# A two-layer decoder on one core: its first stages reordered, gate products turned round, out_proj and the next norm in one stage

## The reference

```python
x = x + mamba_int8(ln(x))       # in_proj, conv of 4 taps, x_proj, dt, scan over 512 tokens, out_proj; all weights and
                                # activations rounded to int8 steps: qa(x, s) = clip(round(x / s), -128, 127)
x = x + cross_attention(ln(x), ctx)   # 16 heads of 128, rms-normed q and k; softmax; out
x = x + sparse_experts(ln(x))   # 8 experts: x @ (W + delta_e), delta_e from atoms at 4096 cells; top 2 of 8 by a gate
x = x + channel_attention(ln(x))      # scores between channels, not tokens
x = x + cross_attention_2(ln(x), ctx) # 16 heads of 32, q and k layernormed by head
x = x + ffn_experts(ln(x))      # 12 experts, top 2 by a gate
```

## Time and profile before

| | us |
|---|---|
| median of 3 runs | 3809.16 (3806.95 to 3812.8) |
| the profiled execution: time, span | 3798.11, 3796.4 |
| PE, weight loads, DVE, ACT, POOL busy | 3303.2 (87%), 1722.7, 2493.5, 1766.4, 1207.5 |
| mean granted clock of TensorE | 0.933 of 2.4 GHz |
| moved by DMA | 332 MB, 88 GB/s |

### The profile page before, as it was taken

How to read it: one execution, slowest core, us unless ns; L and a number is a source line. 1 busy time by engine, 2 the same in 40 slices (tenths; PEclk the granted TensorE clock), 3 DMA queues, 4 the chain that set the end, 5 groups by cost and what they waited for, 6 DMA issues and landing times. The chain is left out here.

```text
span 3796.4 us, 38397 instructions
## 1 busy us (share of the span) xinstructions
PE 3303.2 (87%) x12729; PEld 1722.7 (45%) x12741; DVE 2493.5 (66%) x4700; ACT 1766.4 (47%) x3318; POOL 1207.5 (32%) x927
## 2 busy tenths in 40 slices
PE   2751499999999799999999999899899779999964
PEld 2330144444444354554555454544444446555552
DVE  7768899999999565555555555533311458777554
ACT  3657566666666243343344333343201237677521
POOL 0243599999998010010000000124580010000014
PEclk9885699999999899999999999799999889999957
DMA  6114434343432222212211111446420110000046
GB/s 214 69 57 135 161 96 137 103 136 105 129 110 67 93 75 64 81 64 73 67 55 55 53 59 34 145 136 210 143 91 3 51 66 1 1 1 1 4 140 218
DMA packets 199893, 332.28 MB, mean 88 GB/s; under 512 B 25488, under 2 KB 76048, under 8 KB 196624
## 3 DMA queue, kind: packets, MB, share of 16 engines
q1 hardware_dynamic: 186624, 296.09, 23.9%
q0 software_dynamic: 12208, 33.57, 3.2%
q10 hardware_dynamic: 864, 0.18, 0.0%
HBM read 216.38 MB, written 113.38 MB: 87 GB/s over the span
## 5 line engine op out<-in xcount | busy, mean ns | idle before, releaser
L1201 POOL TENSOR_TENSOR sc_dBu<-sc_dtu,xa 128x1024 f32<-128x1024 f32 x256 | 539.9, 2131 | 41.2 <-DMA sc_dtu<-scan_dtu 32.0
L1111 PE MATMUL y_ps<-sc_g,ident 128*128 128x512 f32 x1024 | 476.3, 600 | 18.4 <-POOL sc_g L1189 12.0
L1225 DVE TENSOR_TENSOR_SCAN sc_dA<-sc_dA,sc_dBu 128x1024 f32<-128x1024 f32 x160 | 365.1, 2282 | 6.3 <-POOL sc_dBu L1201 6.3
L1451 ACT ACTIVATE c_p<-c_ps,c_sm 128x512 f32<-128x512 f32 x256 | 195.6, 774 | 353.4 <-DVE c_sm L1492 353.4
L1165 ACT ACTIVATE sc_dA<-sc_dt,a_neg 128x511 f32<-128x511 f32 x512 | 329.5, 676 | 11.0 <-DVE sc_g L1225 9.8
L1491 DVE TENSOR_REDUCE c_sm<-c_ps 128x4 f32<-128x2048 f32 x64 | 146.7, 2292 | 275.6 <-PE c_ps L1414 275.6
L1111 PEld LDWEIGHTS y_ps<-sc_g,ident 128*128 128x128 f32 x1024 | 189.8, 190 | 256.5 <-issue 168.1
L1484 DVE SCALAR_TENSOR_TENSOR xa<-c_ps,c_sm,xa 128x512 f32<-128x512 f32 x256 | 192.1, 751 | 146.3 <-PE c_ps L1405 132.7
L1405 PE MATMUL c_ps<-c_wo,c_oT 128*128 128x512 f32 x512 | 246.5, 605 | 2.3 <-DVE xa L1484 1.6
L1386 PE MATMUL c_ps<-c_xT,c_wq 128*128 128x512 f32 x512 | 232.3, 597 | 5.3 <-DMA c_wq<-in_c_wq_dram 5.3
L1433 PE MATMUL c_ps<-c_pT,c_v 128*128 128x512 f32 x512 | 232.1, 596 | 1.7 <-DVE c_pT L1503 1.7
(11 more groups left out here) (496 smaller groups left out, 6421.8 us busy)
## 6 DMA issues: line engine op xcount, KB each, us to landing
kv_w<-in_c_wkv_dram SPq DMA_DIRECT2D x32, 512.0 KB, 4.1
cross_keys<-kv_out SPq DMA_DIRECT2D x64, 256.0 KB, 2.0
cross_values<-kv_out SPq DMA_DIRECT2D x128, 128.0 KB, 1.9
c_kT<-cross_keys SPq DMA_DIRECT2D x64, 256.0 KB
c_rk<-cross_rk SPq DMA_DIRECT2D x64, 256.0 KB
c_v<-cross_values SPq DMA_DIRECT2D x64, 256.0 KB
expert_rows<-e_yt SPq DMA_DIRECT2D x63, 256.0 KB, 2.0
xa<-scan_bc SPq DMA_DIRECT2D x48, 256.0 KB, 7.6
```

The costliest lines, as they stand in the source:

```text
L1111: ins = pe.matmul(yps[:, k % 2, :], ident[:], g[:, c % GS, n, :], start=False, stop=(m == NCH - 1 and n == NG - 1))
L1201: pool.tensor_tensor(dBu[:, c % 3], spread(dtu[:, k % DT, :], NG), bc[:, m * NG:(m + 1) * NG, :], ALU.mult).then_inc(s_dBu, 1)
L1225: dve.tensor_tensor_scan(to.rearrange("p n s -> p (n s)"), dA[:, c % 2].rearrange("p n s -> p (n s)"), dBu[:, c % 3].rearrange("p n s -> p ...
L1451: ins = act.activation(pr[:, j, :], ps[:, SB + j, :], ACT.Exp, scale=rq[:, j:j + 1], bias=bias[:, j:j + 1], accum_out=l[:, j:j + 1])
```

## The change

It edits most stages up to qkv1 and leaves scan, heads1 and experts1 as they were. In words, with the core of the diff behind:

1. rsqrt takes three steps, four in entry and x_proj.
2. In the gated norms the gate rows are stationary and 512 tokens move: four products for each batch into `gps`, a copy by DVE (`kept`), four small transposes (`placed`) into the place where the logits were.
3. entry: the raw loads of in_proj_conv move here, SP and ACT split the small loads, conv_w has its own semaphore; `eq` comes ahead of quantized(0), stats(0) and (1) ahead of quantized(1), the weight product's factor ahead of quantized(2); POOL's select waits for tile 0; x is rounded to bf16 and turned as bf16; the raw weights' largest values are taken in the loop at tiles 3, 6, 10 and 13.
4. in_proj_conv: scales at step 0, rounding a step earlier, POOL's cell adds at once; DVE's first pass writes bf16, its second reads and writes bf16.
5. out_proj and norm c0 are one stage with a new class `Norm`; `gqk` is made there, `ones` by POOL in cross0. The ring of products is 4.
6. xT of cross0, the weights of attn1, the context tiles of experts0 and kT of cross1 lie in the memory of `u`, which stays for the whole program. wT is loaded behind heads(1) in cross0.
7. experts0: EARLY = (2, 6, 6).
8. attn1's POOL also centres c1_wq (four tiles) and c1_bq and stores them; qkv1 loads them centred. TURNS alternates keys and queries; project(b + 1) and squares(b + 1) come ahead of both turns of b, keyed(b) behind normalise(b).

```diff
-    for _ in range(4):
+    for _ in range(steps):
...
-                def logits(t):
-                    gw, _, lps = gate
...
-                    copied(t)
-                    for c in range(HC):
-                        pe.matmul(lps[:, t * ne:(t + 1) * ne], xT[:, c, t * P:(t + 1) * P], gw[:, c, :],
+                def logits(b):
...
+                    for t in range(b * TT, (b + 1) * TT):
+                        copied(t)
+                    for c in range(HC):
+                        ins = pe.matmul(gps[:, b % 2, :], gw[:, c, :], xT[:, c, b * S:(b + 1) * S], start=(c == 0),
+                                        stop=(c == HC - 1))
+                    ins.then_inc(s_lg, 1)
+                def placed(b):
+                    pe.wait_ge(s_le, b + 1)
+                    for t in range(b * TT, (b + 1) * TT):
+                        pe.transpose(gate[2][:, t * ne:(t + 1) * ne], lgT[:, b % 2, t % TT * P:(t % TT + 1) * P],
+                                     ident[0:ne, 0:ne])
...
+    def measured(self, dve, own, t):
+        own.after(dve.bn_stats(self.st[:, t, :], self.xa[:, t, :]))
+        own.after(dve.bn_aggr(self.mv[:, t, :], self.st[:, t, :]))
...
-                dve.wait_ge(s_small, 96)
+                dve.wait_ge(s_cw, 16)
...
-                quantized(0, near[:, 0, :], raw[:, 0:WC], W_IN, wq[:, 0, :])
                 dve.wait_ge(s_idxb, 16)
                 dve.tensor_tensor(eq[:], along(idxf[:], P), idxb.rearrange("p (i q) -> p i q", q=P),
                                   ALU.is_equal).then_inc(s_eq, 1)
...
+                quantized(0, near[:, 0, :], raw[:, 0:WC], W_IN, wq[:, 0, :])
+                stats(0)
+                stats(1)
                 quantized(1, near[:, 1, :], raw[:, WC:2 * WC], W_IN, wq[:, 1, :])
-                stats(0)
+                dve.wait_ge(s_del, 1)
+                dve.wait_ge(s_sig, 1)
+                dve.tensor_tensor(wt[:].rearrange("p i e -> p (i e)"), ip[:, 1, 0:ST * NE0],
...
                 pool.wait_ge(s_eq, 1)
+                pool.wait_ge(s_done, 1)
...
-                        own.after(dve.tensor_scalar(v, v, -128.0, 127.0, ALU.max, ALU.min))
-                        dve.tensor_scalar(v, v, MAGIC, MAGIC, ALU.add, ALU.subtract).then_inc(s_xn, 1)
+                        own.after(dve.tensor_scalar(v, xn[:, t % 2, :], MAGIC, MAGIC, ALU.add, ALU.subtract))
+                        dve.tensor_scalar(v, v, -128.0, 127.0, ALU.max, ALU.min).then_inc(s_xn, 1)
...
                 pool.memset(hs[:, :, :, 0:PAD], 0.0).then_inc(s_pad, 1)
-                pool.wait_ge(s_mx, 1)
-                pool.partition_all_reduce(mxa[:], mx[:], P, ABSMAX).then_inc(s_mxa, 1)
                 add_cells(pool, rmw, s_sum, 0, CELL_STEPS[0])
...
-                    own.after(dve.tensor_scalar(v, v, MAGIC - 128.0, MAGIC + 127.0, ALU.max, ALU.min))
...
+                    own.after(dve.tensor_scalar(to, v, MAGIC, 127.0, ALU.subtract, ALU.min))
+                    dve.tensor_scalar(to, to, -128.0, None, ALU.max).then_inc(s_d, 1)
...
                 for t in range(NB * TT):
-                    if t >= 8:
-                        pe.wait_ge(s_out, t - 7)
+                    if t >= 4:
+                        pe.wait_ge(s_out, t - 3)
...
+                    if t >= TT + 2:
+                        norm.turned(pe, t - TT - 2)
+                for t in range(NB * TT - TT - 2, NB * TT):
+                    norm.turned(pe, t)
...
+                        dve.wait_ge(s_out, t + 1)
+                        norm.measured(dve, own, t)
+                    norm.scales(dve, own, b)
+                    if b == 0:
+                        kept()
...
-EARLY = (2, 6, 8)
+EARLY = (2, 6, 6)
...
-                    if n == EARLY[2] + 2:
+                    if n == EARLY[2]:
                         pe.wait_ge(s_ye, TL)
...
-    TURNS = [("k", 0), ("k", 1), ("q", 0), ("k", 2), ("q", 1), ("k", 3), ("q", 2), ("q", 3)]
+    TURNS = [("k", 0), ("q", 0), ("k", 1), ("q", 1), ("k", 2), ("q", 2), ("k", 3), ("q", 3)]
...
-            turned("k", 0)
             project(0)
-            turned("k", 1)
-            for b in range(1, NB):
-                project(b)
-                turned("q", b - 1)
+            for b in range(NB):
                 if b + 1 < NB:
-                    turned("k", b + 1)
-            turned("q", NB - 1)
+                    project(b + 1)
+                turned("k", b)
+                turned("q", b)
...
-            keyed(0)
-            own.after(centre(bq[:], NH1))
-            centre(wq[:].rearrange("p c n -> p (c n)"), HC * NH1).then_inc(s_wq, 1)
-            keyed(1)
             for b in range(NB):
                 taken(b)
                 normalise(b)
-                if b + 2 < NB:
-                    keyed(b + 2)
+                keyed(b)
```

More of the change, by code:

```diff
@@ L159, in _ @@
                         dve.tensor_copy(*out(t - 2)).then_inc(s_ed, 1)
+                    if gate is not None and t >= 8 and t % TT == 0:
+                        kept(t // TT - 2)
+                if gate is not None:
+                    kept(NB - 1)
             @block.scalar
@@ L198, in _ @@
                     ins.then_inc(s_tr, 1)
-                    if gate is not None and t >= 3:
-                        logits(t - 3)
+                    if gate is not None and t >= 6 and (t - 6) % TT == 0:
+                        logits((t - 6) // TT)
+                    if gate is not None and t >= 8 and t % TT == 0:
+                        placed(t // TT - 2)
                 if gate is not None:
-                    for t in range(NT - 3, NT):
-                        logits(t)
+                    logits(NB - 1)
@@ L218, with mamba @@
 CELLS = H * H
-def mamba(nc, A, x_dram, xa, u, gate, owq, dtq, zero, rmw, soft, sgd, bcd, kv, ident, identb):
+def mamba(nc, A, x_dram, xa, u, gate, owq, dtq, zero, rmw, soft, sgd, bcd, kv, gqk, ident, identb):
     with ExitStack() as ctx:
@@ L1518, with experts0 @@
 HALVES = 2 * NB * TT
-EARLY = (2, 6, 8)
-def experts0(nc, A, d, rows, parts, xa, ident, held, raw_kv):
+EARLY = (2, 6, 6)
+def experts0(nc, A, d, spare, rows, parts, xa, ident, held, raw_kv):
     NTT = NB * TT
@@ L2166, in _ @@
             own = Order(dve, s_own)
-            def centre(w, n):
-                heads = w.rearrange("p (h d) -> p h d", d=HD)
-                own.after(dve.tensor_reduce(mw[:, 0:n], heads, AX_X, ALU.add))
-                own.after(dve.tensor_scalar(mw[:, 0:n], mw[:, 0:n], 1.0 / HD, None, ALU.mult))
-                return dve.tensor_tensor(heads, heads, along(mw[:, 0:n], HD), ALU.subtract)
             def keyed(b):
@@ L2677, in program @@
             zero = c2.enter_context(nc.sbuf_tensor("zero", [P, S], F32))
-            mamba(nc, A, x_dram, xa, u, gate, owq, dtq, zero, rmw, soft, sgd, bcd, (keys, values, rkd), ident,
-                  identb)
+            mamba(nc, A, x_dram, xa, u, gate, owq, dtq, zero, rmw, soft, sgd, bcd, (keys, values, rkd), gqk,
+                  ident, identb)
         with ExitStack() as c2:
             d = c2.enter_context(nc.sbuf_tensor("e0_d", [P, HC, NE0, H], F32))
-            cross0(nc, A, xa, ident, table, d, keys, values, rkd)
-            experts0(nc, A, d, rows, parts, xa, ident, ctx, raw_kv)
+            cross0(nc, A, xa, spare, gqk, ident, table, d, keys, values, rkd)
+            experts0(nc, A, d, spare, rows, parts, xa, ident, ctx, raw_kv)
         with ExitStack() as c2:
             kst = c2.enter_context(nc.sbuf_tensor("k1_st", [P, 3, NB * TT * NH1], F32))
-            attn1(nc, A, xa, ident, raw_kv, kn, vn, kst)
-            cross1(nc, A, xa, ident, kn, vn, kst)
+            attn1(nc, A, xa, spare, ident, raw_kv, kn, vn, kst, wqc)
+            cross1(nc, A, xa, spare, ident, kn, vn, kst, wqc)
         experts1(nc, A, rows, parts, xa, out.rearrange("b (j p) c -> p (b j) c", p=P), ident, ctx)
```

351 lines of the change are left out of this document (213 added, 138 removed).

## The result

The changed kernel takes 3749.67 us (median of 4 runs, 3742.67 to 3752.61) where the kernel before takes 3808.05 (3794.75 to 3812.8) in the same set: 0.9855, with a 95% interval of 0.9827 to 0.9883. The forecast was 3760, faster. The profiled execution has a span of 3740.9 us, 55.5 less than before's 3796.4; both lie some 10 us under their medians, so the difference of the two traces comes near that of the medians, 58.4.

A forecast was written before the change was run, and what follows sets the result against it. Bounds were read stage by stage: PE fills cross0; DVE, ACT and PE share in_proj_conv beside POOL's adds; norms and qkv1 are chains with gaps. Terms sum to -49: 3749 us profiled, 3760 median, range 3739 to 3785.

The forecast's parts named there:

- the product's place: Entry: issuing the weight product earlier lets the first copy of x follow the scales in 3 to 4 us, -12.5.
- the loop: Entry: DVE gets the raw weights' reductions, 7 us, costing 3 to 4 beyond its slack, +3.5 in the sum.
- the end of -18: Entry: the most favourable end of its forecast range, -18 to -10, around -15 us.
- POOL is late next: in_proj_conv: POOL's cell adds at 8.5 us each end the stage at 118, the other chain at 110 to 117.
- the end of -10: Norm e1: the most favourable end of its forecast range, around -8 us.
- the 1.2 GHz rival: Merged stage and both gate norms: transposes don't count as busy, so the clock stays at 1.2 GHz; 3802, chance 0.06.
- (a): in_proj_conv: POOL's adds go faster once the queues are empty of weight loads, -6: 3754; chance 0.13.
- (b): Entry and qkv1 give less, +5 and +4, with experts0's late products at +8: 3771; chance 0.22.
- (c): Merged stage and both gate norms: the clock stays at 1.2 GHz, 3802, inside 0.2%; chance 0.06.
- (d): in_proj_conv: DVE's denser bf16 passes hold back POOL's adds, up to 62 us: 3822, slower; chance 0.04.
- (e): Norms e0 and e1: placement transposes cost as much as what they replace, no gain: 3772; chance 0.07.
- The upper side of 3785: Whole kernel: the forecast range's slow end, said to be reached by (b), (e) and half of (c).

The follow-up runs named there:

- e6: Changed kernel with entry's weight product moved back behind the scales and conv_w's rounding: 3761.0 us beside 3817.1 for the kernel before; entry 109.8.
- e3: Changed kernel with POOL's cell adds in in_proj_conv held until DVE's second step is finished: 3740.6 us beside 3803.2 for the kernel before; stage 124.2.
- e1: Changed kernel with EARLY back at (2, 6, 8) and batch 2's context loaded ahead of the tiles: 3728.4 us beside 3803.2 for the kernel before.
- e7: Changed kernel with qkv1 in nearly the old order, centred weights kept: 3739.4 us beside 3817.1 for the kernel before; qkv1 90.2.
- e8: Changed kernel with EARLY = (2, 8, 8) and batch 2's context loaded ahead of the tiles: 3746.5 us beside 3817.1 for the kernel before; experts0 250.4.
- e10: Changed kernel with eight places instead of three for experts0's late keys and values: 3752.7 us; experts0 258.4.
- e12: Changed kernel with EARLY = (2, 8, 8), eight places for late keys and values, and qkv1's keys scaled and turned ahead: 3735.2 us, 0.9809 of before.
- e4: Changed kernel with out_proj, norm c0 and gqk apart again, three root steps: 3730.5 us beside 3803.2 for the kernel before; the pieces 58.5.
- e9: The changed kernel word for word, timed again as yardstick: 3752.12 us against 3807.6 for the kernel before, 0.9849.
- e11: Changed kernel with EARLY back at (2, 6, 8) and batch 2's context loaded ahead of the tiles, timed: 3746.0 us, 0.9836 of before.
- e0: Not a run but a stage, the gated norm between cross0 and experts0: 43.9 us in the kernel before, 38.6 in the changed kernel.
- e2: Kernel before with only the gate products turned round in the gated norms, four root steps: 3775.2 us beside 3803.2 for the kernel before.
- e5: Changed kernel with in_proj_conv's two DVE passes in f32 as before: 3747.6 us beside 3817.1 for the kernel before; stage 120.8.

## Why the prediction was right, and where its steps were not

**Entry, -15 forecast, -18.6 measured.** All parts were right in kind. The first xn came 7.8 us earlier instead of 6; the first copy of x 3.2 us behind the scales, as foreseen; and e6 prices the product's place at 11.8 of the 12.5. The term mis-sized is the loop: from the first copy to the stage's end it was 19.5 us (99.67 to 119.2) and is 21.7 (78.97 to 100.6), so the reductions cost 2.1 beyond the slack and not 3.5. The rest of the difference is in the first xn. The -18.6 lies beyond the end of -18.

**in_proj_conv, -19 and -20.5** (-18 to -21 over all runs). Right size, wrong chain, so the size is partly luck. The step that failed is "POOL is late next": it took the adds at their 8.5 us each of the earlier trace rows, and they run at 7.8, ending 9 us before the stage. The chain of PE, ACT and DVE decides. I had put its end at 110 to 117, and it came at 112.1 into the stage, but without the 4.6 us until SP's last store lands, which the forecast gave to POOL's chain alone. The second pass takes 0.69 us where I took 0.94 from a row of 1248 columns. The two errors nearly cancel. The 5.6 us that the forecast puts behind the last gather's start are 6.9 by the trace (249.4 to 256.3), a small slip. e3 says how near the two chains are: the adds have some 5 us of slack. The runs show one thing more: the faster the adds, the longer the stage. With 7.35 to 7.42 us an add (e1, e7, e8, e10, e12) it takes 118.0 to 118.9, with 7.8 (changed, e4, e9) 116.7 to 117.0, with 8.0 (e6, e11) 115.9 and 116.0. A bound by the adds would go the other way.

**Merged stage, -1.5 and -1.6.** The sum came out, its reading didn't: apart (e4) the pieces take 58.5. I took DVE's chain for its length, which was right, and set it against the old total; I did not see that merging by itself gives nothing and that all of the gain is root steps.

**cross0, 0 and +0.9.** As worked out.

**Norms e0 and e1, -4 and -8; -5.4 and -11.6.** Mechanism right, and e2 shows it alone. The size was off by the clock: I took full speed for half of each, and it was granted at 0.87; e1's -11.6 lies beyond the end of -10. The gated norms can't say whether transposes alone hold the clock up, since after the change these stages have wide products too. The norms without a gate can. Norm a1 of e4, in two stretches, where PE has only the 64 transposes:

```profile
2617.00:2629.80 12.80, 3.58 (x16) 3.14 (x16) 12.14 (x37) 4.45 (x7) 0.00 (x0) 0.50 0.90 318
2629.90:2642.60 12.70, 7.57 (x49) 5.03 (x48) 8.53 (x30) 10.70 (x18) 0.00 (x0) 1.00 0.29 90
```

The granted clock rose to 2.4 GHz behind sixteen transposes at 1.2 and stayed there for the other 48. The Trainium skill, TensorE: Matmul & The Clock Gate, Part 4: PE-mode transpose, by whose rule I held the 1.2 GHz rival open, says that the full clock doesn't engage for transposes; this trace and the earlier trace rows show otherwise. For the gated norms the rows show that swapping narrow products for wide ones took the granted clock from 0.52 to 0.87.

**experts0, +6 and +9.5.** This term was short of a mechanism. The reordering itself came out at +2.5 to +3 where there were no gaps (241.5 and 242.0 against 239.0), with 4.8 between the two values of EARLY inside one set, while e2, which has the old order, took 237.9 in that set. The head gained 5.6 (4 to 5 forecast); the two products cost 7.0 in the tail, and from the first tile to the first late product it is 1.9 longer (1.3 forecast, for the evacuation). The further 7.0, 65.6 us for the late products instead of 58.6, hang on the 6.9 in which ACT waits for a late store. The trace of before had no such gap, and neither a term nor a rival named it; over the runs the late products lose up to 18 us by it. With it the stage passes the end of +8.

**qkv1, -6 and -6.5.** Both parts right: PE projects from the first microsecond (-13 forecast), and 20.2 us stand behind DVE's last take-up, of which e7 gives 5.3 back, the +5 of the working.

**Small stages.** The norms a1 and c1 gained 2.3 for 1.2 forecast; in e2, with four root steps and the rest of before's norm a1 and c1, each is already 0.6 shorter, so the steps give about what was said and the rest isn't theirs. heads1's -2.4 is also in e2 (475.1), where no stage from qkv1 to heads1 is changed: it isn't an effect of the change's parts there. Its first products run at 1.2 GHz, which the row of before shows,

```profile
3138.60:3148.90 10.30, 10.30 (x48) 5.99 (x50) 7.32 (x25) 5.65 (x13) 0.00 (x0) 0.50 0.00 1
```

with PE busy for all of it, and this stretch ends 21.3 us into the stage in before, 17.1 in e2 and 16.3 in the changed kernel. attn1's +1.7 is of the same kind, and no term had it: the changed kernel's first products there have a stretch of 3.4 us at 1.2 GHz,

```profile
2650.70:2654.10 3.40, 3.40 (x6) 1.34 (x5) 0.00 (x0) 0.00 (x0) 0.00 (x0) 0.50 0.76 231
```

and so has e9, the same kernel once more; both take 316.0. In the other twelve traces the clock is 1.00 for all of attn1, and it takes 314.3 or 314.4. Why it falls there is open.

**The rivals.** (a) was true in its fact, the adds go faster, and false in its time, since they no longer come last. (b), give-backs in entry and qkv1, did not happen; only its late products did. (c) is false: none of its three stages stayed at 1.2 GHz. (d), POOL starved by denser DVE passes, went the opposite way: bf16 passes let the adds go at 7.35 to 8.0 us each, and the f32 passes of e5 hold them at 8.45. The rows show how. Two scatters, issued 0.3 us into DVE's second pass, first in the changed kernel, then in e5:

```profile
206.43 0.69 DVE L781 TENSOR_SCALAR gate<-gate 128x2048 bf16<-128x2048 bf16 x1
206.72 1.26 POOL L621 DMA_INDIRECT sparse_table<-new,locu  x1 [0.28 <-POOL new L619]
```

```profile
214.93 1.23 DVE L781 TENSOR_SCALAR u<-xa 128x2048 bf16<-128x2048 f32 x1
215.23 1.79 POOL L621 DMA_INDIRECT sparse_table<-new,locu  x1 [0.28 <-POOL new L619]
```

The pass is 0.54 us longer and so is the issue, 1.79 instead of 1.26; an issue that meets no pass takes 0.97. What counts is how long each pass is, and not how dense DVE's work looks. The Trainium skill, SBUF — State Buffer, section SBUF: two separate sides, says that DVE in a two-port mode holds the shared port pair for the whole instruction, and that GpSimd can't write descriptors meanwhile. The traces agree with it, with 1.26 and 1.79 us beside passes of 0.69 and 1.23. The wait behind the pass is shown; that the port is what is waited for wasn't tested by itself. (e) is false; the placement transposes are cheap. The upper side of 3785 isn't the sum of what it names: 11, 12 and half of 42 would give 3804; nothing measured comes near it.

## What to carry to other kernels

A product that stands in an in-order queue ahead of a critical turning costs nearly its full length (11.8 of 13.8 us here), and a turning is free only in a gap of its engine: read the order of each queue, not its busy share. When a stage's bound goes, list every chain's end down to the last landing store, as two chains 5 us apart can swap places without the forecast's total showing it. Where a stage ends in a tail full of transfers, its time varies by more than a reordering moves it (241.5 to 260.0 here), so compare it over several executions, stage by stage.

## What the runs showed of the hardware that I had not expected

- A DVE pass from bf16 to bf16 over 2048 columns takes 0.69 us, from f32 1.23; and with the shorter one POOL's gather, add and scatter beside it take 7.35 to 8.0 us instead of 8.3 to 8.5 (eleven kernels against three). An indirect DMA that POOL issues while a pass runs takes longer by about what is left of the pass (1.26 and 1.79 us with 0.40 and 0.93 left, 0.97 with none).
- With narrow products (8 and 12 columns, a new stationary tile each) the norms had a granted clock of 0.63 and 0.52; with the gate's rows stationary and 512 columns moving it was 0.87, in the same stages with the same transposes.
- Stores of one form land within 10 us or far later in the same code of experts0: in e3 and e4 a copy starts at most 10.1 us behind the store it waits for, in e9 up to 21. In e9 the DMA engines are then busy 0.8 of the time and carry 252 and 277 GB/s, in e4 1.0 and 325 to 368. The cause is open.
- With transposes alone on PE, 16 at 1.2 GHz, the granted clock rose to 2.4 GHz and stayed for the 48 that followed (norm a1 of e4).
